# Two attentions: rotating PSUM banks and re-spread layer norms in the first, earlier turned maxima in the second

## The reference, cut to what matters

```python
xn = _layernorm(x)
s = _L0_attn_ref(xn, ...)        # 16 heads of 8, causal, + xn, then a layer norm with gamma, beta
g = _silu(_L0_ffn_ref(xn, ...))
x = x + s * g
xn = _layernorm(x)
s = _L1_attn_ref(xn, ...)        # 16 heads of 64, causal, output projection
g = _silu(_L1_ffn_ref(xn, ...))  # eight experts, two per token
x = x + s * g
```

## Time and profile before

| | us |
|---|---|
| median of 3 runs | 3430.91 (3429.36 to 3445.45) |
| the profiled execution | 3440.53 |
| its span, first to last instruction | 3438.8 |
| PE busy | 2857.1 (83%) |
| DVE busy | 2400.6 (70%) |
| ACT busy | 1628.2 (47%) |
| POOL busy | 1651.4 (48%) |

### The profile page before, as it was taken

The page is one execution under the profiler, slowest core; times in us unless marked ns, Lnnn a source line. Parts: engine busy times, 40 slices in busy tenths (PEclk is TensorE's granted clock), DMA queues, the critical chain, the costliest instruction groups (busy, mean ns, idle before and its releaser), DMA issues. The chain is left out here.

```text
span 3438.8 us, 63418 instructions
## 1 busy us (share of the span) xinstructions
PE 2857.1 (83%) x20023; PEld 1761.7 (51%) x20037; DVE 2400.6 (70%) x5517; ACT 1628.2 (47%) x2647; POOL 1651.4 (48%) x1635
## 2 busy tenths in 40 slices
PE   0045489888888896799999999999999996999998
PEld 0024233333333332566666666666666665888787
DVE  8978367777777674566666666666666665887877
ACT  3434335454445443444544444545544443555554
POOL 4546412121212111355555555555555554888887
PEclk9987579888989887799999999999999998999999
DMA  1000122222131211011101110111101112232231
GB/s 49 0 6 0 44 74 73 82 64 93 53 94 57 78 62 41 14 36 36 32 29 35 35 35 29 36 35 35 32 30 35 35 54 90 91 98 88 95 94 62
DMA packets 174530, 177.61 MB, mean 52 GB/s; under 512 B 33840, under 2 KB 126065, under 8 KB 174322
## 3 DMA queue, kind: packets, MB, share of 16 engines
q1 hardware_dynamic: 174336, 175.47, 16.5%
HBM read 121.77 MB, written 43.12 MB: 48 GB/s over the span
## 5 line engine op out<-in xcount | busy, mean ns | idle before, releaser
L1667 DVE CUSTOM_DVE_ANT_0 a_scored<-a_pMax,a_causal 128x128 bf16<-128x128 f32 (+3 forms) x1024 | 451.9, 485 | 462.2 <-PE a_pMax L1835 462.2
L1010 DVE TENSOR_REDUCE a_max<-a_pMax 128x2 f32<-128x1024 f32 (+3 forms) x512 | 403.8, 821 | 230.0 <-PE a_pMax L624 131.2
L944 ACT ACTIVATE a_PT<-a_pST 128x1024 f32<-128x1024 f32 (+1 forms) x384 | 338.6, 882 | 401.3 <-PE a_pST L624 251.4
L1580 ACT ACTIVATE a_PT<-a_pST 128x1024 f32<-128x1024 f32 (+1 forms) x384 | 338.8, 882 | 381.3 <-PE a_pST L1825 370.2
L1529 POOL TENSOR_SCALAR_AFFINE_SELECT a_PT<-a_PT 128x256 f32<-128x256 f32 x512 | 203.3, 409 | 631.7 <-ACT a_PT L1580 601.2
L2092 POOL TENSOR_TENSOR m_silu<-m_silu,m_cw 128x512 f32<-128x512 f32 x256 | 402.9, 1597 | 125.3 <-ACT m_silu L2130 125.3
L877 POOL TENSOR_TENSOR a_att<-a_att,a_rows 128x512 f32<-128x512 f32 x16 | 20.2, 1265 | 658.9 <-DVE a_att L1071 658.9
L2170 DVE TENSOR_TENSOR m_hT_low<-m_hT,m_hT_high 128x512 fp32r<-128x512 f32 x256 | 275.4, 1076 | 78.3 <-ACT m_hT_high L2117 78.2
L1843 PE MATMUL a_pO<-a_PT,a_V 128*64 128x512 f32 (+3 forms) x2048 | 324.5, 462 | 0.7 <-POOL a_PT L1529 0.7
L2130 ACT ACTIVATE m_silu<-m_pG 128x512 f32<-128x512 f32 x256 | 153.0, 599 | 211.0 <-PE m_pG L2210 200.7
L1547 POOL TENSOR_TENSOR a_SM<-a_PT 128x768 f32<-128x768 f32 x128 | 235.0, 1836 | 10.6
(11 more groups left out here) (296 smaller groups left out, 6946.8 us busy)
## 6 DMA issues: line engine op xcount, KB each, us to landing
a_rden<-inverse_sums_dram SPq DMA_DIRECT2D x256, 128.0 KB, 2.9
m_cw<-cw_dram SPq DMA_DIRECT2D x32, 1024.0 KB, 5.5
a_KS<-k_parts_dram SPq DMA_DIRECT2D x64, 224.0 KB
a_QS<-q_parts_dram SPq DMA_DIRECT2D x64, 192.0 KB
a_xn_staged<-xn SPq DMA_DIRECT2D x32, 256.0 KB, 3.3
a_max_rows<-a_mT SPq DMA_DIRECT2D x512, 2.0 KB
q_parts_dram<-a_parts SPq DMA_DIRECT2D x16, 384.0 KB, 2.6
k_parts_dram<-a_parts SPq DMA_DIRECT2D x16, 384.0 KB
```

Of the source, the lines that this page charges most:

```text
L944: a.activation(PT[p][:, :, at:at + w], pST[:, :, 0:w], ACT.Exp, scale=SCALE).then_inc(exped.sem, 1)
L1010: last = v.tensor_reduce(MX[:, :, p, j], pMax[(NM * p + m) % 2][:, :, at:at + (j + 1) * P], AX.X, ALU.max, negate=True)
L1580: a.activation(PT[s.q % 2][:, :, k * TOK:k * TOK + w], pST[:, :, 0:w], ACT.Exp, scale=SCALE).then_inc(exped.sem, 1)
L1667: last = v.tensor_tensor_reduce(scored[:, cc, at:at + w], pMax[:, cc, at:at + w], causal[:, TOK - w:], -1.0, 3e38, ALU.add, ALU.min, MX[pa ...
```

## The change

In attention0 `pST` and the two `pMax` become three double banks that rotate: score round k uses bank 2k mod 3, max round m bank 2m+1 mod 3, so that the sequence score, max, score, max takes banks 0, 1, 2, 0, 1, 2. A max round now waits for the exponential of the score round before this one, and a score round waits for the reductions of the max round two before. The layer norms are cut in fifteen pieces (eight and seven) and spread over both units: `normalise` has pieces 0 to 4 in the second half of the even unit and 5 to 7 in the first half of the odd one; `normalise_x1` has 0 to 4 in the second half of the odd unit and 5, 6 at the start of the next even one. GpSimd's `residual` moves from the end of the even unit to the odd unit, ahead of the two `split`s. In attention1 `turn_m` moves from behind the second max round to behind the first, and `m_evac` from behind the second exponential to behind the first.

```diff
+    AHEAD = NM * LEAD
-        pMax = [ps(f"pMax{i}", [P, 2, TOK]) for i in range(2)]
-        pST = ps("pST", [P, 2, TOK])
+        banks = [ps(f"pair_banks{i}", [P, 2, TOK]) for i in range(3)]
+        score_bank, max_bank = [banks[2 * k % 3] for k in range(NS)], [banks[(2 * m + 1) % 3] for m in range(NM)]
...
+                    if n.odd and not n.no_before:
+                        residual(step, n.b - 1, 1 - n.parity)
                     if n.prepare:
                         split(step, n.b + 2, 0, q_in, q_parts)
-                    if n.prepare:
                         split(step, n.b + 2, 1, k_in, k_parts)
-                    if not n.odd and not n.no_before:
-                        residual(step, n.b - 1, 1 - n.parity)
...
             def normalise(step, b, parity, piece):
                 A = ATT[parity]
                 if piece == 0:
                     o_in.wait(v, 4 * b + 3)
                     step.then(v.tensor_tensor(A[:], A[:], XN[:, bass.ds(b * TB, TB), :], ALU.add))
+                elif piece == 1:
                     tile_stats(step, A, 1e-8)
-                elif piece == 1:
+                elif piece == 2:
                     variance(step)
-                elif piece == 2:
-                    newton(step, 2)
+                elif piece == 3:
+                    seed(step)
+                elif piece < 7:
+                    newton(step)
                 else:
-                    newton(step, 1)
                     for t in range(TB):
...
+                    def norm(*pieces):
+                        if not n.no_before:
+                            for piece in pieces:
+                                normalise(step, b - 1, 1 - n.parity, piece)
+
+                    def norm_x1(*pieces):
+                        back = 1 if n.odd else 2
+                        if not (first and s <= 2):
+                            for piece in pieces:
+                                normalise_x1(step, b - back, (n.parity + back) % 2, piece)
                     lead(0, 1)
+                    if n.odd:
+                        norm(5)
+                    else:
+                        norm_x1(5)
                     lead(0, 2)
+                    if n.odd:
+                        norm(6)
+                    else:
+                        norm_x1(6)
                     lead(1, 0)
+                    if n.odd:
+                        norm(7)
...
                     lead(2, 1)
+                    if n.odd:
+                        norm_x1(0)
+                    else:
+                        norm(0)
                     lead(2, 2)
+                    if n.odd:
+                        norm_x1(1)
+                    else:
+                        norm(1)
                     lead(3, 0)
+                    if n.odd:
+                        norm_x1(2, 3)
+                    else:
+                        norm(2)
                     lead(3, 1)
+                    if n.odd:
+                        norm_x1(4)
+                    else:
+                        norm(3, 4)
                     lead(3, 2)
...
+            for piece in (5, 6):
+                normalise_x1(step, NB - 2, 0, piece)
...
             def max_round(u, par, pair, p, m):
-                bank = pMax[(NM * p + m) % 2]
-                maxed.wait(pe, n - 2)
+                bank = max_bank[m]
+                if isinstance(n, int) and n <= AHEAD:
+                    maxed.wait(pe, n - 3)
+                else:
+                    exped.wait(pe, n - AHEAD - 1)
...
             def score_round(u, par, pair, p, k):
-                exped.wait(pe, NS * (PAIRS * u + p) + k - 1)
+                n = NS * (PAIRS * u + p) + k
+                if isinstance(n, int) and n - 2 + AHEAD >= NM * PAIRS * NU:
+                    exped.wait(pe, n - 3)
+                else:
+                    maxed.wait(pe, n - 2 + AHEAD)
...
@@ attention1, scalar
                     exp(s, 0)
+                    if s.turn_m:
+                        m_evac(s.r + 1)
                     if not s.start:
                         o_evac(s.r - 1, (q - 1) % PB)
...
                     exp(s, 1)
-                    if s.turn_m:
-                        m_evac(s.r + 1)
@@ attention1, tensor
                     score_round(s, 0)
                     maximum(0)
+                    if s.turn_m:
...
+                        turn_m(r + 1)
                     if not s.start:
...
                         weigh(before, range(TB))
...
                     score_round(s, 1)
                     maximum(1)
-                    if s.turn_m:
...
-                        turn_m(r + 1)
```

More of the change, by code:

```diff
@@ L943, in exp @@
                 at, w = k * TOK, WIDTH[k]
-                a.activation(PT[p][:, :, at:at + w], pST[:, :, 0:w], ACT.Exp, scale=SCALE).then_inc(exped.sem, 1)
+                a.activation(PT[p][:, :, at:at + w], score_bank[k][:, :, 0:w], ACT.Exp, scale=SCALE).then_inc(exped.sem, 1)
             def o_evac(n):
@@ L1009, in maxima @@
                 for j, at in MAXB[m]:
-                    last = v.tensor_reduce(MX[:, :, p, j], pMax[(NM * p + m) % 2][:, :, at:at + (j + 1) * P], AX.X, ALU.max, negate=True)
+                    last = v.tensor_reduce(MX[:, :, p, j], max_bank[m][:, :, at:at + (j + 1) * P], AX.X, ALU.max, negate=True)
                 last.then_inc(maxed.sem, 1)
@@ L1049, in variance, with seed, newton @@
                 step.then(v.tensor_tensor(mv[:, :, 1], mv[:, :, 1], t4[:], ALU.add))
+            def seed(step):
                 step.then(v.tensor_scalar(y4[:].bitcast(I32), mv[:, :, 1].bitcast(I32), -0.5, RSQRT_SEED, ALU.mult, ALU.add))
-            def newton(step, rounds):
-                for _ in range(rounds):
-                    step.then(v.scalar_tensor_tensor(t4[:], y4[:], -0.5, y4[:], ALU.mult, ALU.mult))
-                    step.then(v.tensor_tensor(t4[:], t4[:], mv[:, :, 1], ALU.mult))
-                    step.then(v.scalar_tensor_tensor(y4[:], t4[:], 1.5, y4[:], ALU.add, ALU.mult))
+            def newton(step):
+                step.then(v.scalar_tensor_tensor(t4[:], y4[:], -0.5, y4[:], ALU.mult, ALU.mult))
+                step.then(v.tensor_tensor(t4[:], t4[:], mv[:, :, 1], ALU.mult))
+                step.then(v.scalar_tensor_tensor(y4[:], t4[:], 1.5, y4[:], ALU.add, ALU.mult))
             def normalise(step, b, parity, piece):
@@ L1081, in normalise_x1 @@
                 elif piece == 2:
-                    newton(step, 2)
+                    seed(step)
+                elif piece < 6:
+                    newton(step)
                 else:
-                    newton(step, 1)
                     v.wait_ge(staged, 16 * (b + 1))
@@ L1116, in lead @@
                             maxima(target[0], target[2], m)
-                    def layer_norm(piece, odd):
-                        if n.odd == odd and not n.no_before:
-                            (normalise_x1 if odd else normalise)(step, b - 1, 1 - n.parity, piece)
+                    def norm(*pieces):
[7 more added lines that the diff above has]
+                                normalise_x1(step, b - back, (n.parity + back) % 2, piece)
                     lead(0, 0)
@@ L1153, in _ @@
             o_normal(step, 2 * NU - 1, NB - 1, 1, 1, 1)
-            for piece in range(4):
+            for piece in (5, 6):
+                normalise_x1(step, NB - 2, 0, piece)
+            for piece in range(8):
                 normalise(step, NB - 1, 1, piece)
-            for piece in range(4):
+            for piece in range(7):
                 normalise_x1(step, NB - 1, 1, piece)
@@ L1196, in score_round @@
                         rows = split_rows(half)
-                        pe.matmul(pST[:, half, at:at + TOK - kb * P], KS[par][rows, pair, kb * P:(kb + 1) * P],
+                        pe.matmul(score_bank[k][:, half, at:at + TOK - kb * P], KS[par][rows, pair, kb * P:(kb + 1) * P],
                                   QS[par][rows, pair, kb * P:TOK], start=(at == 0), stop=False)
                 for half in range(2):
-                    mm = add_far(pe, pST[:, half], [at for at, _ in ROUNDS[k]], far, identb)
+                    mm = add_far(pe, score_bank[k][:, half], [at for at, _ in ROUNDS[k]], far, identb)
                 mm.then_inc(st_ready.sem, 1)
@@ L1924, in turn @@
                     maximum(0)
+                    if s.turn_m:
+                        if s.next_x:
+                            xT_in.wait(pe, b + 1)
+                        elif q == PB - 2 and not last:
+                            l_in.wait(pe, b + 1)
+                        else:
+                            qk_low.wait(pe, 2 * (r + 2) + 1 if s.max else NR * 2 - 1)
+                        turn_m(r + 1)
                     if not s.start:
@@ L1933, in turn @@
                     maximum(1)
-                    if s.turn_m:
-                        if s.next_x:
-                            xT_in.wait(pe, b + 1)
-                        elif q == PB - 2 and not last:
```

(4 more changed lines are left out.)

10 lines of the change are left out of this document (1 added, 9 removed).

## The result

The changed kernel takes 3299.91 us (median of 4 runs, 3296.33 to 3303.31), the kernel before 3430.14 beside it: ratio 0.9605, interval 0.9571 to 0.964, 130 us less. The profiled execution took 3296.33 us, its span 3294.6 against 3438.8; these two are 144 us apart, since the one of before lies 10 us above its median.

What follows compares the result with a forecast made beforehand. Waits between engines, with no engine full, were taken to bound the kernel. Terms -33 + 15 - 10 - 15 - 4 + 2 + 0 gave -45 us: profiled 3395.5, median 3386 us, range 3330 to 3440.

Steps and rivals of the forecast that it cites:

- Fifteen pieces over both units: attention0's layer norms: smaller, spread pieces remove a quarter of TensorE's 41.6 us late stops; -10 us, bounds +20 and -41.6.
- The clock: TensorE in attention0: fewer stops raise the mean clock by 0.018; -15 us, bounds +40 and -57.
- attention1: Earlier turn and copy there shorten only waits nobody depended on; the 69.6 us stay; 0, bounds -5 and +5.
- Rotating banks, the exponential: attention0: score rounds no longer wait for the exponential just before them; -33 us, bounds 0 and -106.
- the reductions: attention0: with rotating banks TensorE stops one score round sooner when VectorE is late; +15 us, bounds 0 and +41.
- GpSimd and SP's queue: attention0's odd units: later residual and splits stay hidden, put_q leaves 2.7 us ahead of m_rows; cost 0.
- Rival C: attention0's odd units end waiting up to 1.5 us for m_rows behind put_q; +21 us, 3407 us; chance 0.08.
- The ends: attention0's last units: four exponential waits go, -4 us, against +2 us for two late layer-norm pieces.
- Rival A: attention0: short, many stops at score rounds drop the clock to 0.80; +36 us, 3467 us; chance 0.13.
- Rival B: attention0: VectorE takes the gain back, TensorE waiting at score rounds for the same reductions; +3 us, 3434 us; chance 0.18.
- Rival D: attention0: waits for exponentials and reductions both go, clock rises to 0.95; about -125 us, 3306 us; chance 0.06.

Runs made afterwards that it cites:

- e1: Kernel before with only attention0's three rotating banks and their waits: 3426.11 us, 0.9968 of before.
- e2: Kernel before with only the fifteen layer-norm pieces and the moved residual in attention0: 3340.6 us, 0.9711 of before.
- e10: Changed kernel with GpSimd's splits on the turns' batches cut from 512 to 32 columns: 3269.2 us, 0.952 of before.
- e11: Kernel before with rotating banks and splits cut to 32 columns, layer norms left in place: 3354.83 us, 0.9769 of before.
- e5: Changed kernel with SP's m_rows in attention1 put ahead of inverses and sums_compact: 3248.39 us, 0.9442 of before.
- e12: Changed kernel with SP's m_rows first in both attentions, so ahead of put_q in attention0: 3244.35 us, 0.9458 of before.
- e3: Kernel before with only attention1's earlier transpose and copy of the maxima: 3447.37 us, 1.0019 of before.
- e4: Changed kernel with attention1 as before, so banks and pieces only: 3308.21 us, 0.9615 of before.
- e13: Kernel before with 8 single-column scratch memsets on VectorE between the two attentions: 3406.09 us, 0.9903 of before.

## Why the prediction was wrong

The direction and the places of the stops were right; the time failed in the terms *Fifteen pieces over both units* and *The clock*, and in *attention1* by something that wasn't in the sum. The sum also went by 14 batches in 820 us, where the row holds 14.7.

- *Rotating banks, the exponential* (-33) and *the reductions* (+15): alone 11 us with all that follows from them, where the two terms gave 18. In the changed kernel the exponential left the score round's waits, 7.2 us came before max rounds (I had said about 11), and the reductions' waits moved to the score round with 40.6 us (I had said no more than 50). That the two rows came near is in part luck: alone (e1) the waits for reductions rose by 60 us, over the bound of 41, and took back all that the exponential's lost. The terms aren't independent of the next: on top of the pieces the banks brought 33.
- *Fifteen pieces over both units* (-10, at best -41.6): the failed step. Measured alone 99 us (0.0289 of 3440), of which 31 lie in attention1 and 55 in attention0 against the mean of five; the profiled execution of e2 was 11 us slower than its median. I expected a quarter of the 41.6 us of late stops to go, and e2 has 2.0 left. I said that add, seed and first Newton rounds of `normalise_x1` would "again be held" by splits: the seed was (563 ns), the others weren't (L1056 went to 162 ns). Of what was held before I priced only L1055, 23 us of 46, and the room that the spread layer norm leaves the reductions counted for more than the hold (e10 against e11). I had read one clustered odd unit and priced what I saw idle in it, and not the 2 us behind at half clock as part of the same cost.
- *The clock* (-15, at best -57): 0.08 higher instead of 0.018, and the busy time of the same matmuls fell by 60 us, four times the term. My rate, 8.2 us a hundredth, was about right (60 / 8 = 7.4); the rise was not derived from the stops, but chosen. It is no term beside the stops: idle time and clock mostly go together in the table, though not strictly, since e1 has more idle time than before at a higher clock.
- *GpSimd and SP's queue* (0): `put_q` 3.1 us ahead of `m_rows` (2.7 forecast), and VectorE never waits at L1041. Rival C isn't borne out: the two stops of 2.79 us for rows in e5 lie at the loop's turns, where e12, with `m_rows` ahead of `put_q`, stops all the same.
- *The ends* (-2) aren't resolved.
- *attention1* (0): right for the edit in its time (e3: 1.0019), and by luck. SP's waits for the copy fell, to 11.3 us, but "the 69.6 us stay" was wrong: 16 of them went, and 15 to 20 us of busy time came, for which I had a bound of 5. e5 shows that `inverses` ahead of `m_rows` makes the rows late, as I said. Wrong for the stage: the place of the code took 31 us off, and I had written that a move of over 10 us would prove me wrong. TensorE's waits for rows fell from 69.6 to 36.2, about half by the place of the code (52 in e2, e4 and e13) and half by the early turn.
- Rival A: the clock rose. The Trainium skill, "TensorE: Matmul & The Clock Gate", section "A second HAM failure mode: psum-queue depth-cycling", spoke for it; rotating banks alone left the clock of the steady stretch at 0.88, and with spread layer norms it was 0.95 and 0.96. Rival B: the banks alone are as it said, in time (11 us) and in mechanism (101.3 us of waits for reductions); the whole change isn't. Rival D, both kinds of waits and the clock at 0.95, gave 3306 for a chance of 0.06: its time was met, by another sum, since the waits for reductions kept their 40 us.

The hold itself was to be had from the Trainium skill, page "SBUF — State Buffer", section "SBUF: two separate sides": GpSimd and VectorE share a pair of ports that whichever starts first holds until its instruction ends, and VectorE asks for it in operations with two SBUF inputs and in its two-port modes. The section "Who interferes with whom" of the same page counts casts among those that can enter such a mode, and reductions not. The traces agree: L1055 (two inputs from SBUF) took 431 ns in the mean and 165 with short splits, after the change the casts took 685 and 361, and the reductions 820 and 821 ns in both kernels. L1054's 158 ns say nothing against it, though it reads `y` twice: in the odd unit shown it starts just ahead of a GpSimd operation (883.75 us against 883.81, 886.14 against 886.17). What sets the cost is which steps meet a GpSimd operation after the move. In the odd unit at 890 us of the changed kernel the last split ends at 900.93 us, the seed is held until 900.95, and the first Newton step starts at 900.98: free.

## What to carry to other kernels

A stop of TensorE costs its idle time and the stretch at half clock behind it; here the two were 53 and 60 us, so price them together. Look for what keeps the engine with the due work (the reductions) from doing it: 46 us of held steps cost 51, and layer norms clustered in half a unit, with the place of `residual`, 66. When a stage that nobody edited changes its length, compare the instruction packets before looking for a reason in the code; and before making a copy earlier, see which queue issues the transfer behind it: two lines of SP's order were worth 51 us, the early turn nothing, and then minus 17. When an edit is worth nothing, compare busy and idle time of the same work: here the nothing was 16 us gained and 15 lost. And count the work in a window before comparing windows.

## What the runs showed of the hardware

The place of a loop's code alone moved attention1 by 31 us of 1439, with 127 instruction packets against 62. A held VectorE step lasts until the GpSimd operation beside it ends, 1.05 us for 0.16. The same 10422 matmuls of attention1, with TensorE idle for 11 and 16 us only, kept it busy for 1345.6 or 1323.9 us, by the place of one small transpose: the weighing started 0.21 us behind it, the projection 0.03.
